# Second pass of an attention and mixture-of-experts block: x2 turned by VectorE over DRAM instead of by TensorE

## The reference

```
q = elu(h @ Wq.T + bq) + 1;  k = elu(h @ Wk.T + bk) + 1;  v = h @ Wv.T + bv     (16 heads of 32)
KV = sum over rows of k (x) v;   Z = 1 / (q . sum(k) + 1e-6)
x = x + ga * ((q KV Z) @ Wo.T + bo)
```

```
V = h @ fWv.T + fbv;   r = V @ Wg.T + bg;   c = for each expert the norm of its 8 probes of V
s = ln(r) + sigmoid(alpha) * ln(c);   w = softmax(top 2 of s)
delta = sum over e of w_e * (silu(V @ W1[e].T + b1[e]) @ W2[e].T + b2[e])
x = x + gb * (V + delta)
```

## Time and profile before

| | |
|---|---|
| median of 3 runs | 1216.82 us (1216.78 to 1216.86) |
| the profiled execution | 1216.84 us, span 1215.1 us |
| PE busy | 1202.4 us, 99% |
| VectorE (DVE) busy | 1001.0 us, 82% |
| ScalarE (ACT) busy | 545.0 us, 45% |
| GpSimd (POOL) busy | 609.1 us, 50% |
| DMA | 131.65 MB, 108 GB/s mean |

### The profile page before, as it was taken

The page is one execution under the profiler, slowest core; times in us unless marked ns, Lnnn a source line. Parts: engine busy times, 40 slices in busy tenths (PEclk is TensorE's granted clock), DMA queues, the critical chain, the costliest instruction groups (busy, mean ns, idle before and its releaser), DMA issues.

```text
span 1215.1 us, 18365 instructions
## 1 busy us (share of the span) xinstructions
PE 1202.4 (99%) x5680; PEld 987.7 (81%) x5680; DVE 1001.0 (82%) x2218; ACT 545.0 (45%) x1127; POOL 609.1 (50%) x458
## 2 busy tenths in 40 slices
PE   8999999999999999999999999999999999999998
PEld 5888878787877787887778888888888888888887
DVE  6988788988889888886788888888887888888775
ACT  4455454454454545454534343443434343443432
POOL 1443433333333443444556575766657576675741
PEclk9999999999999999999999999999999999999999
DMA  6565544444343343443231322313232231322201
GB/s 225 166 192 180 159 129 143 139 138 125 111 131 107 119 129 120 124 139 112 79 96 61 96 77 81 104 53 104 63 95 88 70 105 53 105 70 88 87 19 53
DMA packets 128515, 131.65 MB, mean 108 GB/s; under 512 B 12233, under 2 KB 82289, under 8 KB 128417
## 3 DMA queue, kind: packets, MB, share of 16 engines
q1 hardware_dynamic: 128416, 130.47, 34.6%
HBM read 80.62 MB, written 49.81 MB: 107 GB/s over the span
## 4 chain that ended last, share of the span: by engine, by line
PE 85%; DVE 5%; issue 4%; ACT 3%; DMA 1%; POOL 1%; SPq 0%; POOLq 0%; DVEq 0%; ACTq 0%
PE ps L1637 26%; PE ps L1638 26%; PE ps L1644 26%; PE ps L1853 3%; PE ps L1845 1%; DMA wm_in<-in_L_wmod_dram 1%; PE ps L1745 1%; DVE zk L1306 1%; DMA q_in<-q_scratch 1%; ACT exp_k L859 1%; ACT exp_q L830 1%; DVE qf L1282 1%; ACT exp_q L832 1%; POOL cn L725 1%; ACT exp_k L861 0%
## 5 line engine op out<-in xcount | busy, mean ns | idle before, releaser
L696 POOL TENSOR_TENSOR xn_lo<-xn,xn_hi 128x512 fp32r<-128x512 f32 x64 | 85.9, 1342 | 279.6 <-ACT xn_hi L821 279.6
L725 POOL TENSOR_TENSOR cn<-c,half 128x16 f32<-128x16 f32 x32 | 104.1, 3254 | 189.8 <-DVE c L1405 189.8
L830 ACT ACTIVATE exp_q<-qf 128x512 f32<-128x512 f32 x64 | 40.5, 632 | 150.5 <-DVE qf L1282 150.3
L1637 PE MATMUL ps<-wk_hi,xT_hi 128*128 128x512 f32 x256 | 101.8, 398 | 2.3 <-ACT xT_hi L815 2.3
L1637 PE MATMUL ps<-g_hi,qT_hi 128*128 128x512 f32 x256 | 103.2, 403 | 0.1
L1637 PE MATMUL ps<-v_hi,xT_hi 128*128 128x512 f32 x256 | 103.0, 402 | 0.0
L1637 PE MATMUL ps<-k_hi,xn_hi 128*128 128x512 f32 x256 | 102.7, 401 | 0.0
L1637 PE MATMUL ps<-wq_hi,xT_hi 128*128 128x512 f32 x256 | 102.5, 400 | 0.1
L1638 PE MATMUL ps<-wq_lo,xT_hi 128*128 128x512 f32 x256 | 101.4, 396 | 0.0
L1638 PE MATMUL ps<-wk_lo,xT_hi 128*128 128x512 f32 x256 | 101.3, 396 | 0.0
L1638 PE MATMUL ps<-k_lo,xn_hi 128*128 128x512 f32 x256 | 100.6, 393 | 0.0
(11 more groups left out here) (250 smaller groups left out, 3333.8 us busy)
## 6 DMA issues: line engine op xcount, KB each, us to landing
xin<-_attn_hidden_states_dram SPq DMA_DIRECT2D x64, 256.0 KB, 3.1
q_scratch<-qf SPq DMA_DIRECT2D x64, 256.0 KB, 3.3
xin<-_attn_hidden_states_dram SPq DMA_DIRECT2D x32, 512.0 KB, 4.2
q_in<-q_scratch SPq DMA_DIRECT2D x128, 128.0 KB, 2.9
out_dram<-qf SPq DMA_DIRECT2D x64, 256.0 KB, 2.0
xn_scratch<-xn SPq DMA_DIRECT2D x62, 256.0 KB, 2.0
xq<-xn_scratch SPq DMA_DIRECT2D x248, 64.0 KB, 2.5
wm_in<-in_L_wmod_dram SPq DMA_DIRECT2D x4, 1024.0 KB, 6.1
```

What stands on the lines that cost most here:

```text
L696: nc.gpsimd.tensor_tensor(moved(xn_lo[:, 1 - s, :], i + 1), kept(xn[:, 1 - s, :], i + 1), moved(f32(xn_hi[:, 1 - s, :]), i + 1), ALU.subtr ...
L725: nc.gpsimd.tensor_tensor(cn[:].rearrange("p h e -> p (h e)"), c2[:].rearrange("p h e -> p (h e)"), half[:], ALU.pow).then_inc(cn_done, 1)
L830: nc.scalar.activation(exp_q[:, s, :], zq[:, s, :], ACT.Relu, scale=-1.0).then_inc(rq_done, 1)
L1637: nc.tensor.matmul(dst, ah, bh, start=start and n == 0, stop=False)
```

## The change

x2 of pairs 3 to 30 is no longer transposed by PE. ScalarE writes it to xn with the 32-column blocks exchanged, SP stores it to DRAM (x2_scratch), waits, and loads it in four quarters into x2q; VectorE transposes it into bank_x2T (turned_x2). Pairs 0, 1, 2 and 31 keep turn_x2. SP loads q three pairs ahead, not two, and den, inverses, qz and turned_q are one pair further ahead; all of the qT_lo of pairs from 3 on are GpSimd's. turn_hidden, aT_high and aT_low take both halves of a pair at once: the first into bank_qaT, the second into bank_x2T, so turn_hidden(j) waits for x2T_low of pair j+1, second tile. PE's order in step j is now out(j,0), out(j,1), fused(j-1,0), turn_hidden(j-2), fused(j-1,1), both expert products of j-2, value(j-1, 0 and 1). On the other engines the lists are rewritten; weights(j-1) now ends VectorE's step j, and GpSimd's q_times_ks waits for it.

```diff
+        FIRST_TURNED, LAST_TURNED = 3, J - 2
+        two_aT = ps[:, 4:6, 0:2 * P]
+        def by_pe(j):
+            return j < FIRST_TURNED or j > LAST_TURNED
@@ SP
+            def x2_store(j, h):
+                sp.wait_ge(x2_done, 2 * j + h + 1)
+                sp.dma_start(x2_dram[rows(2 * j + h), :], xn[:, h, :]).then_inc(x2_out[h], 16)
+            def x2_load(j, h):
+                sp.wait_ge(x2_out[h], 16 * (j - 2))
+                wait_count(sp, x2T_turned, 2 * (j - 4) + h + 1)
+                for i in range(KB):
+                    sp.dma_start(x2q[DH * i:DH * (i + 1), h, :].rearrange("p (g f) -> p g f", f=P),
+                                 x2_dram[rows(2 * j + h), i * P:(i + 1) * P].rearrange("(g t) f -> t g f", t=DH)).then_inc(x2_back[h], 16)
             def step_b(j):
+                if live(j + 3, J):
+                    sp.wait_ge(qz_done, j + 2)
+                    q_load(j + 3)
+                if j > 2 and live(j + 1, J):
                     sp.wait_ge(xb_done, j + 1)
                     bx_load(j + 1)
+                if live(j, J) and not by_pe(j):
+                    for h in range(2):
+                        x2_store(j, h)
+                        x2_load(j, h)
+                        result_store(j - 2, h)
...
@@ GpSimd, from step 3
             def step_b(j):
                 if live(j + 2, J):
+                    pool.wait_ge(aw_done, j - 1)
                     q_times_ks(j + 2)
+                if live(j + 1, J):
+                    queries_low(j + 1)
                 if live(j, J):
                     row_scale(j)
+                probe_norms(j - 1)
+                router_scale(j - 1)
                 if live(j + 1, J):
                     biased_x(j + 1)
@@ ScalarE
+            def aT_high(j):
+                act.wait_ge(aT_psum, j + 1)
+                wait_count(act, y_psum, 2 * j)
+                nc.scalar.copy(wT_hi[:], bank_qaT[:, 2 * P:3 * P])
+                nc.scalar.copy(aT_hi[:], two_aT).then_inc(aTh_done, 1)
...
                 act.wait_ge(shift_done, j + 1)
+                dst, src = (xn[:, h, :], x1_of(j, h)) if by_pe(j) else (quarters(xn[:, h, :]), natural(x1_of(j, h)))
...
@@ ScalarE, order of step j > 3
+  qT_high(j + 1, 0); deviations(j, 0); x2T_high(j - 1, 1); qT_high(j + 1, 1); deviations(j, 1); variances_eps(j)
+  aT_high(j - 2); den_plus_eps(j + 2); functions(j - 1); normalised(j, 0); normalised(j, 1)
+  x2T_high(j, 0); exponentials(j - 1)
@@ VectorE
+            def turned_x2(j, h):
+                dve.wait_ge(x2_back[h], 64 * (j - 2))
+                dve.wait_ge(x2Tl_done, 2 * j + h)
+                dve.wait_ge(aTl_done, j - 1)
+                nc.vector.transpose(bank_x2T.rearrange("p (j g t) -> p g j t", j=KB, g=KB),
+                                    x2q[:, h, :].rearrange("p (g j f) -> p g j f", g=KB, j=KB)).then_inc(x2T_turned, 1)
@@ VectorE, order of step j > 3
+  residual(j, 0); turned_x2(j - 1, 1); residual(j, 1); x2T_low(j - 1, 1); denominators(j + 2)
+  biased(j - 1, 0); aT_low(j - 2); inverses(j + 2); biased(j - 1, 1); probes(j - 1); gated(j - 1)
+  finished(j - 2, 0); scaled_q(j + 2); finished(j - 2, 1); variances(j - 1); turned_q(j + 2)
+  turned_x2(j, 0); x2T_low(j, 0); scores(j - 1); weights(j - 1)
@@ PE
+            def turn_hidden(j):
                 pe.wait_ge(aw_done, j + 1)
+                wait_count(pe, aTl_done, j)
+                pe.wait_ge(x2Tl_done, min(2 * j + 4, T))
+                nc.tensor.transpose(bank_qaT[:, 2 * P:3 * P], ws[:], ident[:])
+                turn(bank_qaT, aw[:, 0, :], 2)
+                turn(bank_x2T, aw[:, 1, :], 2).then_inc(aT_psum, 1)
...
+                    out_product(j, 1)
+                fused_product(j - 1, 0)
+                turn_hidden(j - 2)
+                fused_product(j - 1, 1)
+                expert_product(j - 2, 0)
+                expert_product(j - 2, 1)
+                value_product(j - 1, 0)
+                if live(j, J) and by_pe(j):
                     turn_x2(j, 0)
+                value_product(j - 1, 1)
```

More of the change, by code:

```diff
@@ L228, in build @@
         qks = sb("qks", [P, 2, D], F32, late)
+        x2q = sb("x2q", [P, 2, D], F32, late)
         den = sb("den", [P, 2, HEADS], F32, late)
@@ L641, in _ @@
             q_load(3)
+            sp.wait_ge(qz_done, 3)
+            q_load(4)
+            sp.wait_ge(xb_done, 3)
+            bx_load(3)
             q_store(T - 1, 1)
@@ L1544, in _ @@
             x2T_low(1, 1)
+            qT_low(2, 1)
+            scores(0)
+            weights(0)
             q_feature(T - 1, 1)
-            scores(0)
+            residual(2, 0)
             denominators(3)
-            weights(0)
-            qT_low(2, 1)
+            inverses(3)
+            residual(2, 1)
             biased(1, 0)
+            aT_low(0)
             biased(1, 1)
-            aT_low(0, 0)
-            inverses(3)
-            scaled_q(3)
             probes(1)
             gated(1)
-            residual(2, 0)
+            finished(0, 0)
@@ L1558, in _ @@
+            scaled_q(3)
+            finished(0, 1)
             turned_q(3)
-            residual(2, 1)
-            aT_low(0, 1)
-            finished(0, 0)
+            variances(1)
+            x2T_low(2, 0)
             denominators(4)
[L1563 to L1566, removed]
             scores(1)
-            qT_low(3, 1)
+            weights(1)
+            inverses(4)
+            x2T_low(2, 1)
             def step_b(j):
[L1571 to L1585, removed]
@@ L1595, in step_b @@
                 if live(j + 2, J):
                     denominators(j + 2)
[L1597 to L1600, removed]
+                biased(j - 1, 0)
+                aT_low(j - 2)
+                if live(j + 2, J):
+                    inverses(j + 2)
+                biased(j - 1, 1)
+                probes(j - 1)
+                gated(j - 1)
+                finished(j - 2, 0)
+                if live(j + 2, J):
+                    scaled_q(j + 2)
@@ L1601, in step_b @@
+                finished(j - 2, 1)
+                variances(j - 1)
+                if live(j + 2, J):
+                    turned_q(j + 2)
+                if live(j, J) and not by_pe(j):
+                    turned_x2(j, 0)
                 if live(j, J):
                     x2T_low(j, 0)
[L1603 to L1618, removed]
-            finished(J - 2, 1)
-            aT_low(J - 1, 0)
-            aT_low(J - 1, 1)
+                scores(j - 1)
+                weights(j - 1)
+            sweep_pairs(step_b, 3, J)
+            aT_low(J - 1)
             finished(J - 1, 0)
@@ L1870, in turn_x2 @@
                 wait_count(pe, x2Tl_done, t)
+                wait_count(pe, aTl_done, j - 1)
                 turn(bank_x2T, xn[:, h, :], KB).then_inc(x2T_psum, 1)
```

170 lines of the change are left out of this document (79 added, 91 removed).

## The result

| | before | after |
|---|---|---|
| median of the runs | 1216.78 us (1216.53 to 1219.4, 11 runs) | 1211.75 us (1210.48 to 1214.84, 11 runs) |
| ratio to before | | 0.9959, 95% interval 0.9952 to 0.9967 |
| the profiled execution | 1216.84 us, span 1215.1 | 1211.52 us, span 1209.8 |

The change makes the kernel 0.41% faster: 5.0 us, where 15 were forecast. 1211.75 us lies inside the range, and is the time of rival 2, but not by rival 2's mechanism: that it fell into the range is luck, since most of the loss came from elsewhere.

A forecast was written before the change was run, and what follows sets the result against it. TensorE (PE), 99% busy, was taken to bound the kernel: 1216.8 - 24.6 (turns) + 5.9 (stalls) + 3 (end) + 0.5 (start) = 1201.6, so 1202 us. The range was 1194 to 1218 us.

The forecast's parts named there:

- rival 2: Second-pass bounce lands as in the first pass, 2.5 to 2.8 us: 18.9 to 19.2 a pair, 1210 to 1219 us; 18%.
- What is taken from PE: Pairs 3 to 30: 56 tiles lose 0.44 us of turns each, 24.6 us; a pair can reach 18.39 us.
- The start ... I give 0.5: Pairs 2 and 3, GpSimd's cn, rrs, xb and qT_lo before out_product(3): 0.5 us, bounds -1 and 2.
- the first of the signs: Sign of being wrong: PE's idle stands in front of an instruction other than the turn of ws.
- PE's stalls, 5.9 us: Second pass: ring 18.6 us against PE's 18.39, so PE waits 0.21 us a pair, 28 x 0.21 = 5.9 us.
- The ring's typical sum: Path from turn_hidden through the DRAM bounce (5.60 us) back to PE, once a pair: 18.57 us, taken as 18.6.
- the last line of the forecast's signs: Signs of being wrong: a GpSimd releaser of PE's idle, or an x2 load landing above 2.8 us.
- The end, 3 us: Last step: turn_hidden 2.9 us later plus 0.3 for the first expert product, taken as 3 us, bounds 0 and 4.
- The waits costed at nothing: Second tile's bounce, with 1.5 us of cover, and GpSimd's wait for aw_done were priced at no cost.
- VectorE's lighter load: With GpSimd resting during the router's scores, s3 falls from 1.19 us to 0.2; VectorE's 17.5 us a pair does not bind.
- rival 3: VectorE and GpSimd lock: cn's pow delays hz by 2.7 us, 20.2 us a pair, 1247 us; 6%.
- rival 1: No stall: second-pass loads land in 1.9 us or less, PE keeps 18.39 us a pair, 1196 us; 22%.

The follow-up runs named there:

- experiment 3: The changed kernel with ScalarE's normalised of the first tile moved ahead of functions: 1203.05 us, ratio 0.9887.
- experiment 5: The changed kernel with x2 of all pairs turned by PE, so the new order without the bounce: 1228.41 us, ratio 1.0093.
- experiment 7: experiment 3 and experiment 2 together, plus step 3's scaled_q(4), turned_q(4) and qT_high(4) moved later, and qT_low(4) put on VectorE: 1198.03 us, ratio 0.9846.
- experiment 8: experiment 7 plus, in step 2, biased_x(3) ahead of row_scale(2) on GpSimd and qT_low(3) on VectorE ahead of denominators(4): 1197.45 us, ratio 0.9840.
- experiment 9: experiment 8 with VectorE's two finished(1, h) of step 3 moved ahead of turned_q(4): 1201.44 us, ratio 0.9867.
- experiment 10: experiment 9 with SP issuing x2_store(3, 0) ahead of q_load(6) and bx_load(4) in step 3: 1199.59 us, ratio 0.9850.
- experiment 4: The changed kernel with one more 0.76 us ScalarE instruction, writing an unread tile, ahead of the first tile's normalised in pairs 3 to 30: 1234.68 us, ratio 1.0140.
- experiment 1: The changed kernel with biased_x(3) moved on GpSimd in front of the wait for aw_done and q_times_ks(4): 1211.84 us, ratio 0.9956.
- experiment 2: The changed kernel with VectorE's last step in the order of the kernel before: 1207.88 us, ratio 0.9927.

## Why the prediction was wrong

The mechanism was right, and the size was off, by three terms that all lean to one side: the start, the end, and PE's stalls. The sum said 1202 us, and these three make the 10 us between it and 1211.75.

- **What is taken from PE**, 56 x 0.44 = 24.6 us: right. Undisturbed pairs take 18.41 us (forecast 18.39), and experiments 3 and 5 give 25.2 us for the turns.
- **"The start ... I give 0.5"** is the step that failed most: it cost 4.9 us, beyond its bound of 2. It was priced from GpSimd's list alone. VectorE was the engine that was late. The old order, too, had scaled_q(4) and turned_q(4) ahead of a residual of pair 3, but PE had its fused and expert products to do meanwhile. In the new one PE does both out_products first, VectorE has qz (2.22 us beside GpSimd's qks, 1.22 in experiment 7) and turned_q (1.25) in front of the second residual, and behind them ScalarE's two qT_high(4) and the deviations of that residual stand in front of aT_hi, for which PE waits 3.74 us; scaled_q(5) and turned_q(5) are in the same step besides. The rest is the clock: PE's work from 646 to 652 ran at 0.50, and the pair took 24.69 - 18.41 - 3.74 = 2.5 us more than its work and its wait. Experiment 5 shows that the bounce has no part in it, experiment 7 that the place of pair 4's q is the cause (scaled_q and turned_q on VectorE with qT_high on ScalarE, which it moves together): that wait falls to 0.29 us. GpSimd's lock is in it with the 1.0 us that qz is longer; experiment 8 gives it no more than 0.6 us in scores(1). That the time follows experiment 7 by 1 us only is because another wait comes up in the same step; that VectorE is too full there for one move to free it is what experiments 8 to 10 point to, and no run shows it alone. A wait of PE in front of another instruction than the turn of ws, as this one, was the first of the signs that the prediction named for being wrong.
- **PE's stalls, 5.9 us**: the 27 pairs of the middle lost 8.2 us to stalls, against 27 x 0.21 = 5.7, and their own 18.41 is 0.02 above the forecast's 18.39: 3.0 us more than forecast. The ring's typical sum was even too long: the first tile's bounce, put at 5.60 us, took 5.34 in the median. But of 28 such bounces 10 took 5.49 to 6.56 us, and behind nine of them PE waits (0.28 to 1.03 us; 5.0 us together, and each of these pairs was some 0.15 us longer than its wait explains). In five of the nine the last load landed in 2.6 to 3.2 us, in two the first load went out late, 2.6 us behind the store, and in two an issue in between was held up. The forecast took one value for the landing and multiplied it by 28. Where a ring has so little slack (0.1 us by experiment 4), early landings give nothing and late ones are paid nearly in full, so the mean excess of the bounces counts and not the median. Landings of single loads were 1.8 / 2.0 / 3.5 us (least, median, longest); six of 224 were above 2.8, against the last line of the forecast's signs.
- **The tenth wait of the middle**, 0.91 us at 1152.31, is no landing: that pair's bounce took 5.35 us. VectorE's last instruction of weights(28) took 1.26 us and not 0.17, and ended with GpSimd's qT_lo. The steps before have q_times_ks, which waits for ws, in front of qT_lo; in step 30 q_times_ks has nothing left to do, and qT_lo meets weights(28). VectorE, then GpSimd, after:
```profile
1147.96 1.26 DVE L1550 TENSOR_TENSOR ws<-wt,ws 128x16 f32<-128x16 f32 x1
```
```profile
1147.63 1.56 POOL L752 TENSOR_TENSOR qT_lo<-qTf,qT_hi 128x512 fp32r<-128x512 f32 x1 [3.40 <-ACT qT_hi L929]
```
Experiments 1 and 2 show the same 1.26 us there.
- **The end, 3 us**: the turn of ws was late as worked out (3.40 us of wait, 0.84 for aT_hi). It cost 5.6 us against 3, beyond its bound of 4, and the low clock behind that wait is 2.2 of these by experiment 2. No step of the prediction asked what a long wait does to the clock.
- **The waits costed at nothing** held in the steady pairs. The second tile's bounce took 5.58 to 7.42 us and stayed covered but for the longest, for which VectorE waited 0.40 us (1017.7). Else VectorE waits for x2q once in each pair from the fourth on, in front of the first tile, and GpSimd releases none of PE's waits.
- **VectorE's lighter load**: right in the middle. The rows that answer to the earlier trace rows, VectorE then GpSimd, after:
```profile
901.68 0.18 DVE L1507 TENSOR_TENSOR s<-rcg,rrs 128x32 f32<-128x32 f32 x1
901.89 0.17 DVE L1510 TENSOR_TENSOR s<-s 128x16 f32<-128x16 f32 x1
...
912.07 0.69 DVE L1483 SCALAR_TENSOR_TENSOR hz<-th,zf 128x512 f32<-128x512 f32 x1 [0.24 <-ACT th L947]
```
```profile
911.91 2.90 POOL L757 TENSOR_TENSOR cn<-c,half 128x16 f32<-128x16 f32 x1 [1.02 <-DVE c L1468]
```
With GpSimd at rest s3 takes 0.17 us and not 1.19, and VectorE is busy 208.83 us of the 260 and not 216.57. hz starts 0.16 us inside cn and keeps its 0.69, so rival 3 is out. By the rule of the Trainium skill (SBUF — State Buffer, "Who interferes with whom") hz would have waited for cn's end; the trace agrees with the rule where GpSimd runs a plain tensor_tensor over wide tiles (1.44 us for 0.18 in experiment 1's rows), not for this pow on 128x16.
- **The rivals**: rival 2's time came about, with landings (2.0 us in the median) close to rival 1's 1.9 and not at rival 2's 2.5. Rival 1 is what experiments 3 and 2 made of the kernel, but for the start: 1198.98 us.

## What to carry to other kernels

When a change closes a ring through DRAM, give the ring slack by taking out of it whatever need not be there (here two ScalarE instructions, 8.7 us), and price its stalls by the mean excess of the landings over the slack. Go through the first and last steps of a rewritten order on every engine, each as its own timetable: they were 10.5 us here, more than the forecast's whole stall. A wait of TensorE of some two to four us cost 1.5 to 2.7 us more in most cases, by the clock it comes back with; shorter waits by themselves did not, two of about 1 us close together did in some executions.

## What the runs showed of the chip

- TensorE's granted clock fell to 0.50 in, or within 1.5 us behind, waits of 4.89 us (experiment 9), 3.74, 3.40, 3.01, 2.68, 2.51 and 2.10 (the last three in experiment 4), 2.03, and 1.93 (experiment 1). It stayed at 1.00 after one of 2.45 us (experiment 7) and after single ones of up to 1.83 (experiment 4). Behind the 1.1 and 0.84 us at the end, which six profiled executions have, it fell in two (experiments 9 and 10): the length of the wait alone doesn't tell it, and executions of one kernel differ. When it fell, TensorE spent three to seven us at the 1.2 GHz level, and it cost 1.5 to 2.7 us: 2.2 at the end of the change (experiment 2), 2.7 in experiment 10, 1.5 at the end of experiment 9.
- A bounce of 128x512 over DRAM, a store of 256 KB and four loads of 64 KB with 32-column blocks exchanged, took 5.26 us at the least and 5.34 in the median from issue to last landing in the first tiles of the change, up to 6.56; behind 1 MB of loads it took 9.3 (experiment 9).
- A short VectorE instruction with two SBUF inputs took up to 1.44 us for 0.18 beside a GpSimd tensor_tensor over wide tiles (1.44, 1.20, 1.21 and 1.26 us in the change), and its usual time beside GpSimd's pow on 128x16.
- One DMA issue in SP's queue may hold the next ones up: three of four loads' issues took 0.31 to 0.43 us and one 1.87 in experiment 9, and the steady pair at 914.80 took 2.05 us for four in place of 1.74.
